# A gathered sum over edges: TensorE goes on by half batches, each behind VectorE's adds

## The chip, the cores and the metric

The kernel runs on one core of one Trainium2 chip. The metric is the device time of one execution, in microseconds (us). The engines are TensorE (PE for matmuls, PEld for weight loads in the profile), VectorE (DVE), ScalarE (ACT), GpSimd (POOL) and SyncE (SP); DMA engines move data between memory and the core.

## What is computed

Four graph layers follow each other on 6250 nodes with 256 features and 100000 edges: two attention layers (GAT and a second form), a transformer-like attention layer, and a graph convolution (GCN) with two convolutions. After each layer its result is added to the input and normalized. The change touches the two convolutions of the last layer, in the reference:

```python
def gcn_conv(x, src, dst, W, b, n):
    h = x @ W
    ...
    msg = h[s] * norm[:, None]
    out = jax.ops.segment_sum(msg, d, num_segments=n)
    return out + b
```

Here `segment_sum` adds up, for every node, the rows of the nodes that have an edge to it. The first convolution has rows of 128 numbers, the second rows of 64.

## The kernel before

The edges are sorted by their target and cut into 832 groups of 128 edges (`NSLOT`), so that all targets of a group lie in one window of 128 nodes. Eight groups are one batch, so a pass over the edges has 104 batches (`NBT`). There are six such passes: four for the attention layers (stages a1e, a2e, be and te in the profile) and two plain sum passes, g1e and g2e, made by `sum_pass` (L1856) with rows of 128 and of 64 numbers.

A sum pass works in this way, batch by batch (t):

- GpSimd (`gather`, L1889) fetches for each of the eight groups the 128 rows of the sources from the table in memory by an indirect DMA, L1893. Its destination is a ring of `RING` = 6 batches. It may fetch batch t once batch t - 6 has been summed (`s_summed`). Each half of a batch (four groups) has a semaphore of its own that tells of the landing.
- ScalarE (`mark`, L1920) makes for each group a 128 x 128 matrix of zeros and ones that says which edge goes to which node of the window: eight activations with Abs (L1923) and one with Relu over the whole batch (L1926), into one of `MARKS` = 4 buffers. It waits until that buffer's former batch has been summed.
- TensorE (`step`, L1902) multiplies each group's matrix by its rows, L1909, in float32. The profile shows two weight loads and two matmuls for each of the eight, so 16 and 16 for a batch. The eight results lie side by side in one of `AHEAD` = 4 buffers of PSUM. TensorE waits for the matrix, for the adds of the batch that had the same PSUM buffer (four batches back), and for the landing of each half. Its last matmul of a batch signals `s_summed`.
- VectorE (`step`, L1936) waits for that signal and adds the eight results to the accumulator in SBUF, each in the window of its group, L1943; each add signals `s_added`. The windows' places come from registers that are loaded for four batches at a time (L1061).

In g2e a part of the dense stage that follows is done beside the sums (class `Beforehand`, L1816): every second batch TensorE also transposes a window of x, ScalarE copies it, TensorE multiplies it by weights, and VectorE copies the product away. The engines' programs are written out batch after batch, in that order; nothing is planned at run time.

Of the kernel before, what the change touches and what calls it, by code (L numbers as in the profile page):

```python
# [1855 lines left out]
def sum_pass(nc, c, stage, order, table, width, acc, spare, beforehand=None):  # L1856
# [3 lines left out]
    RING, AHEAD, MARKS, U = 6, 4, 4, 4  # L1860
    with ExitStack() as stack:
# [19 lines left out]
        with nc.Block() as block:  # L1881
# [5 lines left out]
            @block.gpsimd  # L1887
            def _(pool):
                def gather(t):  # L1889
                    r = t % RING  # L1890
                    wait(pool, s_summed, t - RING + 1)
                    for k in range(8):
                        pool.indirect_dma_start(  # L1893
                            out=rows[:, r, k, :], out_offset=None, in_=table,
                            in_offset=bass.IndirectOffsetOnAxis(ap=order.row[:, t * 8 + k:t * 8 + k + 1], axis=0),
                        ).then_inc(s_rows[r][k // 4], 16)

                batches(pool, gather)

            @block.tensor  # L1900
            def _(pe):
                def step(t):  # L1902
                    r, u, b = t % RING, t % AHEAD, t % MARKS
                    pe.wait_ge(s_onehot, t + 1)
                    wait(pe, s_added, (t - AHEAD + 1) * 8)
                    for k in range(8):
                        if k % 4 == 0:
                            pe.wait_ge(s_rows[r][k // 4], t // RING * 64 + 64)
                        last = pe.matmul(ps_u[u][:, k * width:(k + 1) * width], onehot[b][:, k, :], rows[:, r, k, :], start=True, stop=True)  # L1909
                    last.then_inc(s_summed, 1)  # L1910
                    if window_at(t, 0) is not None:
# [7 lines left out]
            def _(act):  # L1919
                def mark(t):  # L1920
# [3 lines left out]
                    act.wait_ge(s_distance, t * 8 + 8)  # L1924
                    wait(act, s_summed, t - MARKS + 1)
                    act.activation(onehot[t % MARKS][:, :, :], distance[:, :, :], ACT.Relu, scale=-1.0, bias=1.0).then_inc(s_onehot, 1)  # L1926
# [6 lines left out]
            def _(dve):  # L1933
                windows = Windows(nc, order, mybir.EngineType.DVE, -8, U)

                def step(t):  # L1936
                    if t == 0:
                        return
                    dve.wait_ge(s_summed, t)
                    for k in range(8):  # L1940
                        mine = acc[:, bass.ds(windows.at(t % U, k - 8) * width, width)]
                        wait(dve, s_added, t * 8 + (k - 8))
                        dve.tensor_tensor(mine, mine, ps_u[(t - 1) % AHEAD][:, k * width:(k + 1) * width], ALU.add).then_inc(s_added, 1)  # L1943
# [1015 lines left out]
```

## Time and profile before

| what | value |
|---|---|
| median of 3 runs | 10409.85 us (10393.64 to 10424.56) |
| the profiled execution's own time | 10424.9 us |
| its span, from first to last instruction | 10423.2 us |
| mean granted TensorE clock | 0.706 of full speed |
| busy: TensorE matmul / VectorE / GpSimd / ScalarE | 6055.0 / 5838.2 / 5885.3 / 4570.6 us |
| g1e, first to last matmul | 7880.2 to 9062.1 us |
| g2e, first to last matmul | 9128.9 to 10316.2 us |

The profile is of one execution. Times are counted from the span's first instruction. Busy time is the time in which an engine works on an instruction; matmuls are pipelined, and the ends of their records are modelled. Idle time of an engine stands before the instruction that it waited for, with what ended the wait, as far as semaphores tell. "issue" means that nothing in the profile ended it. The granted clock is 0.50 (1.2 GHz) or 1.00 (2.4 GHz) at any moment; a figure between is a mean over a stretch.

### The profile page before, as it was taken

How to read it: one execution, taken by the hardware profiler on the slowest of the kernel's cores; microseconds unless marked ns; L12 is line 12 of the kernel's file. 1: busy time of each engine (PE TensorE's matmuls, PEld its weight loads, DVE VectorE, ACT ScalarE, POOL GpSimd, SP SyncE). 2: the span in 40 equal slices, each digit the busy share in tenths (PEclk: the TensorE clock that was granted, in tenths of full speed). 3: DMA queues.
4: the chain of work that ended last, by engine and by line, in shares of the span. 5: the costliest groups of instructions: out<-in, count | busy, mean ns of one | idle time of the engine just before them, and what ended most of it. 6: DMA issues, size and time to landing. Idle time of an engine off the chain costs nothing. (4 is left out here: it accounts for less than half of the span.)

```text
span 10423.2 us, 138279 instructions
## 1 busy us (share of the span) xinstructions
PE 6055.0 (58%) x32739; PEld 4141.4 (40%) x32739; DVE 5838.2 (56%) x17354; ACT 4570.6 (44%) x14076; POOL 5885.3 (56%) x6036
## 2 busy tenths in 40 slices
PE   5775566666556656565555567888873323333434
PEld 3443344444433333343333334555553222323333
DVE  8997566666555555564544568899982212211113
ACT  6996222222344444443222226777753323223332
POOL 7996455554444444425666615666655666466664
PEclk8998666666566666667666688899886555555556
DMA  1332333332222222223333325666641111111111
GB/s 52 117 105 87 107 100 98 97 99 82 61 64 64 66 74 64 62 68 103 107 107 106 107 90 167 177 181 181 179 132 45 47 46 47 40 26 23 23 24 37
DMA packets 518562, 902.79 MB, mean 87 GB/s; under 512 B 149378, under 2 KB 258844, under 8 KB 517404
## 3 DMA queue, kind: packets, MB, share of 16 engines
q0 software_dynamic: 226304, 550.69, 20.1%
q1 hardware_dynamic: 291484, 343.26, 10.8%
q8 instruction: 305, 5.00, 0.2%
q14 instruction: 469, 3.84, 0.1%
HBM read 820.41 MB, written 73.07 MB: 86 GB/s over the span
## 5 line engine op out<-in xcount | busy, mean ns | idle before, releaser
L1263 POOL DMA_INDIRECT all_Y<-table,all_row x3328 | 3212.0, 965 | 2817.5 <-DVE all_Y L1546 1482.1
L1893 POOL DMA_INDIRECT all_Y<-table,all_row x1664 | 1570.0, 943 | 825.0 <-issue 488.2
L1318 PE MATMUL be_ps_u<-all_Y,be_onehot 128*128 128x258 f32 x1664 | 669.8, 539 | 511.3 <-issue 260.9
L1909 PE MATMUL g1e_ps_u<-all_Y,g1e_onehot 128*128 128x128 f32 x1664 | 364.4, 351 | 830.7 <-issue 746.0
L1318 PE MATMUL a1e_ps_u<-all_Y,a1e_onehot 128*128 128x264 f32 x1664 | 788.1, 609 | 48.6 <-DVE all_acc L1558 47.6
L1943 DVE TENSOR_TENSOR all_acc<-all_acc,g1e_ps_u 128x128 f32 x832 | 238.8, 287 | 966.8 <-DMA all_window<-kept_window_dst 745.9
L1558 DVE TENSOR_TENSOR all_acc<-all_acc,be_ps_u 128x258 f32 x832 | 350.8, 422 | 604.2 <-remote 395.2
L1318 PEld LDWEIGHTS be_ps_u<-all_Y,be_onehot 128*128 128x128 f32 x1664 | 377.5, 258 | 755.0 <-issue 650.1
L1909 PEld LDWEIGHTS g1e_ps_u<-all_Y,g1e_onehot 128*128 128x128 f32 x1664 | 317.5, 261 | 877.6 <-issue 810.2
L1318 PE MATMUL te_ps_u<-all_Y,te_onehot 128*128 128x264 f32 x1664 | 586.6, 463 | 97.1 <-DVE all_Y L1538 59.8
L1943 DVE TENSOR_TENSOR all_acc<-all_acc,g2e_ps_u 128x64 f32 x832 | 183.5, 221 | 817.9 <-DMA table<-g2l_tile 383.1
L1318 PE MATMUL a2e_ps_u<-all_Y,a2e_onehot 128*128 128x66 f32 x1664 | 375.8, 363 | 448.7 <-DVE all_acc L1558 344.9
L1909 PE MATMUL g2e_ps_u<-all_Y,g2e_onehot 128*128 128x64 f32 x1664 | 309.8, 325 | 481.7 <-issue 454.5
L717 ACT ACTIVATE all_X<-all_Y,all_acc 128x128 f16<-128x128 f16 x784 | 239.6, 387 | 718.6 <-DVE all_acc L701 660.7
L747 PE MATMUL a2e_rank_ps_p<-all_X 128*128 128x512 f16 (+1 forms) x1568 | 545.2, 509 | 1.1 <-issue 0.9
L1297 PE MATMUL te_ps_q<-all_X,te_turned 128*128 x1664 | 490.1, 432 | 65.6 <-DVE te_product L1601 42.2
L1318 PEld LDWEIGHTS a2e_ps_u<-all_Y,a2e_onehot 128*128 128x128 f32 x1664 | 312.4, 262 | 515.5 <-issue 499.2
L649 POOL TENSOR_SCALAR all_acc<-all_Y,all_acc 128x128 f16<-128x128 f16 x392 | 488.8, 1258 | 45.4 <-DVE all_acc L636 35.4
L1909 PEld LDWEIGHTS g2e_ps_u<-all_Y,g2e_onehot 128*128 128x128 f32 x1664 | 313.0, 259 | 490.1 <-issue 471.1
L1318 PEld LDWEIGHTS a1e_ps_u<-all_Y,a1e_onehot 128*128 128x128 f32 x1664 | 424.1, 288 | 139.8 <-DVE all_Y L1546 52.1
L1484 ACT ACTIVATE be_onehot<-be_distance 128x1024 f32<-128x1024 f16 x104 | 109.9, 1057 | 842.0 <-PE be_ps_u L1318 739.2
L1926 ACT ACTIVATE g1e_onehot<-g1e_distance 128x1024 f32<-128x1024 f16 x104 | 109.9, 1057 | 815.5 <-DMA all_window<-kept_window_dst 752.0
(568 smaller groups left out, 16478.9 us busy)
## 6 DMA issues: line engine op xcount, KB each, us to landing
all_Y<-table,all_row POOLq DMA_INDIRECT x4992
a1e_place_row<-places_dst SPq DMA_DIRECT2D x104, 256.0 KB
a2e_place_row<-places_dst SPq DMA_DIRECT2D x104, 256.0 KB
be_place_row<-places_src SPq DMA_DIRECT2D x104, 256.0 KB
te_place_row<-places_src SPq DMA_DIRECT2D x104, 256.0 KB
all_Y<-lows_dst SPq DMA_DIRECT2D x98, 256.0 KB
all_Y<-codes_dst SPq DMA_DIRECT2D x98, 256.0 KB
all_acc<-lows_src SPq DMA_DIRECT2D x98, 256.0 KB
```

Of the source, the lines that this page charges most:

```text
L649: pool.tensor_scalar(self.row1[b][:, k, :], self.kept.half16, self.row[b][:, k:k + 1], self.kept.other_t[:, t * 8 + k:t * 8 + k + 1], ALU. ...
L717: act.activation(self.row1[b][:, k, :], self.kept.half16, ACT.Sign, bias=self.row[b][:, k:k + 1]).then_inc(self.s_valued, 1)
L747: last = pe.matmul(ps[:, 0:a1 - a0], self.row1[b][:, k, :], self.column1[b][:, k, a0:a1], start=first, stop=final)
L1263: pool.indirect_dma_start(out=rows[:, r, k, :], out_offset=None, in_=table, in_offset=bass.IndirectOffsetOnAxis(ap=order.row[:, t * 8 + k: ...
L1297: last = pe.matmul(ps_q[pair % 2][:, j * HC:(j + 1) * HC], turned[b][:, k * P:(k + 1) * P], queries[:, bass.ds(windows.at(windows_j, chunk ...
L1318: pe.matmul(ps_u[k % 4][:, 0:R], onehot[b][:, k, :], rows[:, t % RING, k, WEIGHT0:value_c0 + HC] if dot else summand[:, b, k, :], start=Tr ...
L1484: act.activation(onehot[b][:, :, :], distance[:, :, :], ACT.Relu, scale=-1.0, bias=1.0).then_inc(s_onehot, 1)
L1558: dve.tensor_tensor(mine, mine, ps_u[k % 4][:, 0:R], ALU.add).then_inc(s_added, 1)
L1893: pool.indirect_dma_start(out=rows[:, r, k, :], out_offset=None, in_=table, in_offset=bass.IndirectOffsetOnAxis(ap=order.row[:, t * 8 + k: ...
L1909: last = pe.matmul(ps_u[u][:, k * width:(k + 1) * width], onehot[b][:, k, :], rows[:, r, k, :], start=True, stop=True)
L1926: act.activation(onehot[t % MARKS][:, :, :], distance[:, :, :], ACT.Relu, scale=-1.0, bias=1.0).then_inc(s_onehot, 1)
L1943: dve.tensor_tensor(mine, mine, ps_u[(t - 1) % AHEAD][:, k * width:(k + 1) * width], ALU.add).then_inc(s_added, 1)
```

## The change

TensorE no longer waits for the batch four back. Before each half of a batch (four groups) it waits until all groups ahead of that half have been added, then for the half's landing, and it signals after each half. VectorE waits for each half's signal before its four adds. `s_summed` thus counts halves, and the waits of GpSimd and ScalarE on it count twice as many; they still stand for whole batches. Buffers, the number of matmuls, adds and gathers, and the work beside the sums in g2e stay the same.

```diff
             def _(pool):
                 def gather(t):
                     r = t % RING
-                    wait(pool, s_summed, t - RING + 1)
+                    wait(pool, s_summed, (t - RING + 1) * 2)
...
                     r, u, b = t % RING, t % AHEAD, t % MARKS
                     pe.wait_ge(s_onehot, t + 1)
-                    wait(pe, s_added, (t - AHEAD + 1) * 8)
-                    for k in range(8):
-                        if k % 4 == 0:
-                            pe.wait_ge(s_rows[r][k // 4], t // RING * 64 + 64)
-                        last = pe.matmul(ps_u[u][:, k * width:(k + 1) * width], onehot[b][:, k, :], rows[:, r, k, :], start=True, stop=True)
-                    last.then_inc(s_summed, 1)
+                    for half in range(2):
+                        wait(pe, s_added, t * 8 + half * 4)
+                        pe.wait_ge(s_rows[r][half], t // RING * 64 + 64)
+                        for k in range(half * 4, half * 4 + 4):
+                            last = pe.matmul(ps_u[u][:, k * width:(k + 1) * width], onehot[b][:, k, :], rows[:, r, k, :], start=True, stop=True)
+                        last.then_inc(s_summed, 1)
...
                     act.wait_ge(s_distance, t * 8 + 8)
-                    wait(act, s_summed, t - MARKS + 1)
+                    wait(act, s_summed, (t - MARKS + 1) * 2)
...
                     if t == 0:
                         return
-                    dve.wait_ge(s_summed, t)
                     for k in range(8):
+                        if k % 4 == 0:
+                            dve.wait_ge(s_summed, (t - 1) * 2 + (k // 4 + 1))
                         mine = acc[:, bass.ds(windows.at(t % U, k - 8) * width, width)]
```

## Rows read from the trace of the kernel before

**Rows 1.** Page, costliest groups: line engine op, out<-in, xcount | busy, mean ns | idle, releaser.

```profile
L1893 POOL DMA_INDIRECT all_Y<-table,all_row x1664 | 1570.0, 943 | 825.0 <-issue 488.2
L1909 PE MATMUL g1e_ps_u<-all_Y,g1e_onehot 128*128 128x128 f32 x1664 | 364.4, 351 | 830.7 <-issue 746.0
L1943 DVE TENSOR_TENSOR all_acc<-all_acc,g1e_ps_u 128x128 f32 x832 | 238.8, 287 | 966.8 <-DMA all_window<-kept_window_dst 745.9
```

**Rows 2.** Line L1893 (gathers): what ended POOL's idle time before it, us, times.

```profile
  issue: 488.2, 1589
  DMA all_window<-kept_window_dst: 145.2, 41
  PE g2e_ps_u L1909: 112.0, 25
  DMA table<-g2l_tile: 37.3, 7
```

**Rows 3.** Tiles g1e_ps_u, g2e_ps_u, be_ps_u: count, min/median/max ns, first and last start.

```profile
L1909 PE MATMUL g1e_ps_u<-all_Y,g1e_onehot x1664: 269/371/583, 7880.2 to 9062.1; 128*128 128x128 f32 x185
L1909 PE MATMUL g2e_ps_u<-all_Y,g2e_onehot x1664: 215/275/476, 9128.9 to 10316.2; 128*128 128x64 f32 x185
L1318 PE MATMUL be_ps_u<-all_Y,be_onehot x1664: 378/508/772, 4773.2 to 6059.8; 128*128 128x258 f32 x185
```

**Rows 4.** Timeline, POOL in g1e: start us, us, instruction [idle before <-releaser].

```profile
8462.45 0.94 POOL L1893 DMA_INDIRECT all_Y<-table,all_row  x1 [5.72 <-DMA all_window<-kept_window_dst]
...
8501.14 0.94 POOL L1893 DMA_INDIRECT all_Y<-table,all_row  x1 [0.31 <-issue]
8507.80 0.94 POOL L1893 DMA_INDIRECT all_Y<-table,all_row  x1 [5.73 <-DMA all_window<-kept_window_dst]
```

**Rows 5.** Timeline, VectorE (DVE) in the same stretch of g1e.

```profile
8462.32 3.29 DVE L1943 TENSOR_TENSOR all_acc<-all_acc,g1e_ps_u 128x128 f32 x8 [12.18 <-DMA all_window<-kept_window_dst]
8467.68 3.30 DVE L1943 TENSOR_TENSOR all_acc<-all_acc,g1e_ps_u 128x128 f32 x8 [2.06 <-issue]
8471.18 1.58 DVE L1943 TENSOR_TENSOR all_acc<-all_acc,g1e_ps_u 128x128 f32 x4 [0.21 <-issue]
```

**Rows 6.** Timeline, TensorE (PE) in the same stretch of g1e.

```profile
8461.42 7.76 PE L1909 MATMUL g1e_ps_u<-all_Y,g1e_onehot 128*128 128x128 f32 x44 [0.33 <-issue]
...
8473.88 0.37 PE L1909 MATMUL g1e_ps_u<-all_Y,g1e_onehot 128*128 128x128 f32 x1 [1.78 <-issue]
...
8506.78 1.50 PE L1909 MATMUL g1e_ps_u<-all_Y,g1e_onehot 128*128 128x128 f32 x4 [0.33 <-issue]
```

**Rows 7.** Timeline, TensorE at the start of g1e: batch 0's second half, then batch 1.

```profile
7885.25 2.08 PE L1909 MATMUL g1e_ps_u<-all_Y,g1e_onehot 128*128 128x128 f32 x8 [2.98 <-DMA all_Y<-table,all_row]
7890.25 2.04 PE L1909 MATMUL g1e_ps_u<-all_Y,g1e_onehot 128*128 128x128 f32 x8 [2.92 <-DMA all_Y<-table,all_row]
7895.20 2.07 PE L1909 MATMUL g1e_ps_u<-all_Y,g1e_onehot 128*128 128x128 f32 x8 [2.91 <-DMA all_Y<-table,all_row]
```

**Rows 8.** Timeline, VectorE at the start of g1e: the adds of batches 0, 1, 2.

```profile
7887.47 3.30 DVE L1943 TENSOR_TENSOR all_acc<-all_acc,g1e_ps_u 128x128 f32 x8 [16.96 <-PE g1e_ps_u L1909]
7921.64 3.29 DVE L1943 TENSOR_TENSOR all_acc<-all_acc,g1e_ps_u 128x128 f32 x8 [30.88 <-DMA all_window<-kept_window_dst]
7961.54 3.30 DVE L1943 TENSOR_TENSOR all_acc<-all_acc,g1e_ps_u 128x128 f32 x8 [36.61 <-DMA all_window<-kept_window_dst]
```

**Rows 9.** Line L1909 by stretch: us, PE busy (x) PEld busy (x), PEclk, DMA share, GB/s.

```profile
7897.30:7921.60 24.30, 8.35 (x31) 7.06 (x32) 0.50 0.20 51
7921.60:7961.50 39.90, 5.67 (x16) 4.61 (x17) 0.50 0.17 44
```

**Rows 10.** Timeline of the attention pass be: TensorE's sums, a gather, VectorE's next add.

```profile
5325.54 3.14 PE L1318 MATMUL be_ps_u<-all_Y,be_onehot 128*128 128x258 f32 x8
...
5333.35 0.95 POOL L1263 DMA_INDIRECT all_Y<-table,all_row  x1 [0.30 <-issue]
...
5334.67 0.42 DVE L1558 TENSOR_TENSOR all_acc<-all_acc,be_ps_u 128x258 f32 x1 [6.97 <-remote]
```

## The prediction

> **What bounds the kernel now.** The change touches one function, so I read the two stages that it makes, g1e and g2e, and leave the other 8,100 us alone: no instruction there is edited. First the costliest groups [rows 1]: the gather's line L1893 keeps GpSimd (POOL) busy for 1570.0 us and idle for 825.0 us; the sums of g1e are 364.4 us of TensorE and its adds 238.8 us of VectorE, both with more idle time than work. Then what ended POOL's idle time [rows 2]: 488.2 us is the 0.30 us between one gather and the next; 145.2 + 112.0 + 37.3 = 294.5 us in 73 waits is POOL standing before a ring slot that has not been summed (the two rows that name a DMA stand for the same wait, since the DMA named was long over). So the pace of a pass is eight gathers of 0.94 + 0.30 us, about 10.0 us for a batch, plus pauses. The first and last matmul of each pass [rows 3] give 1181.9 / 104 = 11.36 us for a batch in g1e and 1187.3 / 104 = 11.42 in g2e, 11.39 on the mean. The timeline of GpSimd [rows 4] shows the pause: 5.72 us, then 32 gathers, then 5.73 us: 45.35 us for four batches.
>
> Why is a slot not summed in time? TensorE's work in a cycle is small: 44 matmul records in a burst of 7.76 us, and then single records 2 to 3 us apart, each with idle time that nothing in the profile ends [rows 6]. The start of the pass tells more. There the matmuls come with the data, 5 us apart [rows 7], and the batch-0 sums, whose last matmuls begin as a group at 7885.25, are added from 7887.47 on [rows 8]. Batch 1's last matmuls run from 7895.20 to 7897.3, but VectorE, idle for 30.88 us, adds them only from 7921.64, and batch 2's from 7961.54. So the sums are done long before the signal of them arrives. Between batch 1's last matmul and its add TensorE took 31 matmuls and 32 weight loads, and in the next 39.9 us 16 and 17 [rows 9]. From this I take a rule of this kernel: while POOL gathers without a break, some number of TensorE instructions are signalled at once, and after that one for each gather. The counts: 64 instructions (two batches of 16 loads and 16 matmuls) by 7921.6, in 41.4 us or 33 gathers, so 31 free ones; then 33 in 39.9 us or 32 gathers. A pause of POOL clears it: after 8501.14 POOL stands still and the burst comes back at about 8506.8 [rows 4, 6]. The pass paces itself in this way: POOL runs ahead until the ring is full, stops, and TensorE's signals come.
>
> The Trainium skill (Perfetto Trace Analysis, Tensor Engine Instruction) says that a matmul's end in the trace is worked out and that its semaphore goes out only when PSUM has acknowledged the write. The trace agrees that the two may differ: under 0.2 us for batch 0, 24 us for batch 1.
>
> **The change part by part.**
> (a) Signals per half, POOL's and ScalarE's waits doubled in count: 104 more increments in each pass, and both still wait for whole batches. Nothing by itself; ScalarE's work for a batch hides in 10 us as before.
> (b) VectorE may add four sums as soon as the half is signalled. The adds (0.43 us apart, eight in 3.30 us, four in 1.58 us [rows 5]) are the same in number. Nothing is saved where POOL sets the pace, as it waits for the end of a batch.
> (c) TensorE's new wait: before a half, all earlier sums must be added. Behind it on TensorE's queue stand that half's 16 loads and matmuls, and in g2e every second batch the transposes and product of the dense stage; for these wait ScalarE's copy and VectorE's keep, and for the sums POOL. A half then costs, from first load to first add, 7887.47 - 7885.25 = 2.22 us [rows 7, 8], plus 1.58 us of adds, plus some 0.1 us from the last add to TensorE's next load (estimated from VectorE's end at 8467.68 + 3.30 = 8470.98, with adds of the next batch 0.2 us behind [rows 5]): 3.9 us at the granted clock of 0.50 (1.2 GHz) that this stretch had [rows 9] and that I keep; 7.8 us for a batch, and with a quarter of the 2.06 us in which VectorE loads its windows [rows 5] 8.3 us. That is less than the gathers' 10.0, so with prompt signals the wait is hidden. Its cover is gone in a pause: what TensorE now does in a burst for nearly three batches, it must then do at 3.9 us a half, and nothing is finished ahead that a pause could signal at once.
>
> The cycle by the rule: POOL resumes when batch m is signalled, with 31 free instructions. Batch m+1 needs 32, is through in 8.3 us, and POOL goes straight on to its second batch, up to 20.0 us. Batch m+2 needs 64 in all; 31 + 16 gathers give 47, so at 20 us about one half of it is through, and POOL stops. The pause: from 0.3 us (in be, the gather of 5333.35 ends at 5334.3 and the add comes at 5334.67 [rows 10]) to 4.7 us (g1e, from 8502.1 to 8506.8 [rows 4, 6]) until signals flow, and then 3.9 to 5.6 us for the half that is left, the latter if the first half's adds are still to come. So 4.2 to 10.3 us of pause behind 20 us: 12.1 to 15.1 us a batch. If some 17 more instructions are free, three batches go between pauses: (30 + 4.2) / 3 = 11.4 to (30 + 10.3) / 3 = 13.4. The ends are 11.4 and 15.1, middle 13.25. The nearest row is the attention pass be, where TensorE is held to a few sums ahead of VectorE: its matmuls span 1286.6 us [rows 3], 12.37 us a batch, and there too VectorE stands idle for 6.97 us in a run of gathers although four sums were computed from 5325.54 to 5328.7 [rows 10]. So holding TensorE back does not free the signals. I take 12.6, nearer to that row.
>
> Sum: 12.6 - 11.39 = 1.21 us, times 208 batches, 252 us. The profiled execution took 10424.9 us, 15 above the median of the runs shown, so 10677 by the profile and 10662 beside the median: I say 10660.
>
> **The rivals.**
> A, faster (chance 0.27). The crawl comes from TensorE's own backlog: it runs up to four batches ahead, its unsignalled instructions pile up, and with at most 16 outstanding they never do. For it: batch 0, with nothing ahead of it, was signalled promptly in the midst of gathers, and batch 1's signal came after 63 further records [rows 8, 9]. Against it: batch 1 too had nothing unsignalled ahead of it, and be's stall has only eight matmuls outstanding [rows 10]. It decides if a lone half is signalled in a run of gathers; then all 294.5 us of POOL's pauses [rows 2] go: 10424.9 - 294.5 - 15 = 10115. The Trainium skill (TensorE: Matmul & The Clock Gate, Architectural detail) gives TensorE a queue of 64 instructions, in which weight loads may pass matmuls. By that page a wait that keeps the queue short would keep it from ever filling; the 63 records agree with such a depth, and the time by it would be rival A's.
> B, no change (0.09): the free instructions are enough for four batches and the pause stays at 5.7 us; 45.4 us for four batches as now, 10410.
> C, far slower (0.05): a half is signalled only in a pause, so that each batch has its own: 10.0 + 4.7 + 3.9 = 18.6 us, 7.2 x 208 = 1500 us more, 11910.
>
> **How the numbers follow.** The forecast has 0.59, with 11.9 to 13.6 us a batch: 106 to 460 us more, 10515 to 10870. Slower by over 0.3% (about what a measurement of this kernel tells from no change) is the forecast and C, less its lowest edge: 0.63. Rival A gives faster, 0.28 with what lies between it and B; same is 0.09. The range leaves out C, the forecast's top, and A's full gain, and reaches down into a partial gain: 10180 to 10860.
>
> **What would show it.** Right: in the middle of g1e POOL pauses every two or three batches, for 5 to 10 us; VectorE's adds come in fours; between them it idles over 5 us while the matmuls of the half have long ended; TensorE's bursts hold 8 records, never 44. The sum of POOL's pauses on L1893 rises from 294.5 to about 550 us. Wrong: POOL at 1.25 us a gather all through with no pauses (A), or pauses of unchanged number and length (B). The forecast falls if a half's adds start within about 2.3 us of its first load throughout the runs of gathers.

## The result, and the profile after

The changed kernel takes 10529.9 us (median of 4 runs, 10514.7 to 10542.9) against 10409.4 for the kernel before: a ratio of 1.0119, 95% interval 1.0102 to 1.0136, or 120.5 us more. The forecast was 252 us more. The direction was right; the size was about twice too large.

Both matmul tiles of the passes, after (answering to [rows 3]; columns: count, min/median/max ns, first and last start):

```profile
L1909 PE MATMUL g1e_ps_u<-all_Y,g1e_onehot x1664: 421/421/583, 7842.3 to 9143.2; 128*128 128x128 f32 x185
L1909 PE MATMUL g2e_ps_u<-all_Y,g2e_onehot x1664: 219/421/476, 9197.5 to 10413.6; 128*128 128x64 f32 x185
```

g1e takes 1300.9 us, 12.51 a batch where the forecast had 12.6; g2e takes 1216.1 us, 11.69 a batch. So in these profiles the passes lost 119.0 and 28.8 us. The profiled executions are 10514.7 and 10424.9 us, 89.8 apart; the 58.0 us between that and the passes' 147.8 are elsewhere, in code that is the same: the first matmul of g1e came 37.9 us earlier here, and over all profiles of this case, whose code up to g1e is the same too, it lies anywhere between 7842 and 7988 us.

The costliest groups of the passes, after (answering to [rows 1]): the adds work as long as before, the sums 428.7 us where it was 364.4, POOL's idle time has grown.

```profile
L1893 POOL DMA_INDIRECT all_Y<-table,all_row x1664 | 1569.9, 943 | 927.4 <-issue 473.8
...
L1909 PE MATMUL g1e_ps_u<-all_Y,g1e_onehot 128*128 128x128 f32 x1664 | 428.7, 439 | 883.8 <-DVE all_acc L1944 461.3
L1944 DVE TENSOR_TENSOR all_acc<-all_acc,g1e_ps_u 128x128 f32 x832 | 238.6, 287 | 1074.3 <-DMA all_window<-kept_window_dst 645.7
```

What ended POOL's idle time before its gathers, after (answering to [rows 2]):

```profile
  issue: 473.8, 1550
  PE g1e_ps_u L1909: 204.2, 31
  DMA table<-g2l_tile: 144.4, 46
  DMA all_window<-kept_window_dst: 47.3, 33
...
  PE g2e_ps_u L1909: 17.0, 2
```

Without "issue", and without the one wait at the start of each pass, these are 412.9 us where 294.5 stood before. Now the middle of g1e after, POOL (gathers that follow a pause; the others come 0.30 us apart), VectorE and TensorE (answering to [rows 4 to 6]):

```profile
8467.38 0.94 POOL L1893 DMA_INDIRECT all_Y<-table,all_row  x1 [7.48 <-PE g1e_ps_u L1909]
...
8488.73 0.94 POOL L1893 DMA_INDIRECT all_Y<-table,all_row  x1 [1.67 <-DMA all_window<-kept_window_dst]
...
8504.53 0.94 POOL L1893 DMA_INDIRECT all_Y<-table,all_row  x1 [6.12 <-PE g1e_ps_u L1909]
```

```profile
8467.25 1.57 DVE L1944 TENSOR_TENSOR all_acc<-all_acc,g1e_ps_u 128x128 f32 x4 [2.28 <-PE g1e_ps_u L1909]
8471.12 1.57 DVE L1944 TENSOR_TENSOR all_acc<-all_acc,g1e_ps_u 128x128 f32 x4 [2.29 <-issue]
8474.98 1.58 DVE L1944 TENSOR_TENSOR all_acc<-all_acc,g1e_ps_u 128x128 f32 x4 [2.28 <-issue]
8478.85 1.57 DVE L1944 TENSOR_TENSOR all_acc<-all_acc,g1e_ps_u 128x128 f32 x4 [2.30 <-PE g1e_ps_u L1909]
8488.60 1.58 DVE L1944 TENSOR_TENSOR all_acc<-all_acc,g1e_ps_u 128x128 f32 x4 [8.18 <-DMA all_window<-kept_window_dst]
8500.55 1.57 DVE L1944 TENSOR_TENSOR all_acc<-all_acc,g1e_ps_u 128x128 f32 x4 [10.37 <-DMA all_window<-kept_window_dst]
8504.40 1.58 DVE L1944 TENSOR_TENSOR all_acc<-all_acc,g1e_ps_u 128x128 f32 x4 [2.27 <-PE g1e_ps_u L1909]
```

```profile
8480.48 2.08 PE L1909 MATMUL g1e_ps_u<-all_Y,g1e_onehot 128*128 128x128 f32 x8 [1.78 <-DVE all_acc L1944]
8490.28 2.05 PE L1909 MATMUL g1e_ps_u<-all_Y,g1e_onehot 128*128 128x128 f32 x8 [7.72 <-issue]
8502.18 2.07 PE L1909 MATMUL g1e_ps_u<-all_Y,g1e_onehot 128*128 128x128 f32 x8 [9.85 <-DVE all_acc L1944]
```

The reader is to see three things. Adds come in fours, 3.86 us apart while signals are prompt (forecast: 3.9). The half summed from 8480.48 to 8482.56 is added only at 8488.60, the next only at 8500.55: late signals, with no crawl of single records, since TensorE may not run ahead. And POOL gathers 16, stops 1.67 us, gathers 8, stops 6.12 us: 37.15 us for three batches, 12.4 a batch. The sums run at the granted clock that the forecast kept, 0.50 (1.2 GHz), by the row of 400 us of g1e (columns as in [rows 9], with the other engines between):

```profile
8200.00:8600.00 400.00, 134.01 (x520) 115.78 (x520) 75.55 (x264) 113.45 (x291) 242.45 (x257) 0.50 0.16 42
```

In the kernel before, the same 400 us had a mean of 0.57, with 0.69 in the stretch from 8461 to 8470 us that holds a burst: there a part ran at 1.00 (2.4 GHz). With the bursts that is gone, and the sums of g1e grew from 364.4 to 428.7 us. It is not what the change costs: spacer_each below has 0.50 there too and takes what the kernel before takes.

In g2e it looks different. POOL and VectorE after:

```profile
9718.01 0.94 POOL L1893 DMA_INDIRECT all_Y<-table,all_row  x1 [3.16 <-DMA table<-g2l_tile]
...
9740.83 0.94 POOL L1893 DMA_INDIRECT all_Y<-table,all_row  x1 [3.16 <-DMA table<-g2l_tile]
...
9763.62 0.94 POOL L1893 DMA_INDIRECT all_Y<-table,all_row  x1 [3.12 <-DMA table<-g2l_tile]
```

```profile
9717.88 1.31 DVE L1944 TENSOR_TENSOR all_acc<-all_acc,g2e_ps_u 128x64 f32 x4 [5.02 <-DMA table<-g2l_tile]
...
9725.21 1.31 DVE L1944 TENSOR_TENSOR all_acc<-all_acc,g2e_ps_u 128x64 f32 x4 [2.17 <-PE g2e_ps_u L1909]
9727.75 0.42 DVE L1853 COPY all_acc<-g2e_ps_o 128x256 f32<-128x256 f32 x1 [1.23 <-issue]
9732.97 1.31 DVE L1944 TENSOR_TENSOR all_acc<-all_acc,g2e_ps_u 128x64 f32 x4 [4.80 <-DMA table<-g2l_tile]
9740.70 1.31 DVE L1944 TENSOR_TENSOR all_acc<-all_acc,g2e_ps_u 128x64 f32 x4 [6.42 <-DMA table<-g2l_tile]
```

A pause of 3.16 us behind every 16 gathers, 47 times in the pass, and no more: when POOL stops, both halves of the batch that it waits for are computed, and only the last signal is owed. My two-batch cycle had a pause of at least 4.2 us here and 10.3 at most.

### The profile page after: what moved, and what is told of

The parts are those of the page before. It is cut to its first block and busy times, and to the rows that moved or that the text cites. A ratio compares the mean times of both kernels' runs of the same rounds, so it can differ in the third digit from the quotient of the medians.

```text
span 10513.0 us, 138695 instructions
## 1 busy us (share of the span) xinstructions
PE 6163.2 (59%) x32739; PEld 4225.8 (40%) x32739; DVE 5847.3 (56%) x17354; ACT 4568.3 (43%) x14076; POOL 5883.5 (56%) x6036
## 3 DMA queue, kind: packets, MB, share of 16 engines
q14 instruction: 471, 3.86, 0.1%
## 5 line engine op out<-in xcount | busy, mean ns | idle before, releaser
L1893 POOL DMA_INDIRECT all_Y<-table,all_row x1664 | 1569.9, 943 | 927.4 <-issue 473.8
L1909 PE MATMUL g1e_ps_u<-all_Y,g1e_onehot 128*128 128x128 f32 x1664 | 428.7, 439 | 883.8 <-DVE all_acc L1944 461.3
L1909 PE MATMUL g2e_ps_u<-all_Y,g2e_onehot 128*128 128x64 f32 x1664 | 381.8, 407 | 702.1 <-DVE all_acc L1944 445.0
L1909 PEld LDWEIGHTS g1e_ps_u<-all_Y,g1e_onehot 128*128 128x128 f32 x1664 | 370.5, 328 | 941.9 <-DVE all_acc L1944 491.3
L1909 PEld LDWEIGHTS g2e_ps_u<-all_Y,g2e_onehot 128*128 128x128 f32 x1664 | 361.6, 316 | 748.0 <-DVE all_acc L1944 462.5
```

The costliest lines, as they stand in the source:

```text
L1893: pool.indirect_dma_start(out=rows[:, r, k, :], out_offset=None, in_=table, in_offset=bass.IndirectOffsetOnAxis(ap=order.row[:, t * 8 + k: ...
```

## The experiments

Ratios are to the kernel before on the same chip, whose median was 10508, 10511, 10528, 10512 and 10384 us in the five sessions. All kernels in one table; the spans are from the first to the last matmul of a pass, by 104 batches; a pause is a gap of over 0.8 us between two gathers in POOL's timeline (the memsets of the later kernels are in it), and the usual ones are given, with the number of gathers ahead of each. A kernel with a time in place of the ratio ran once. In first_ring_only, two_of_four, sp_loads, uncoupled and half_rows some of the work is left out, or rows are summed that are not the edges'.

| kernel | time, ratio (95%) | g1e, g2e us a batch | usual pauses in g1e; g2e, us |
|---|---|---|---|
| before | 1 | 11.36, 11.42 | 1.5 to 3.0 behind 24, then 3.0 to 4.4 behind 8, or 5.7 behind 32; 4.5 behind 24 |
| changed | 1.0119 (1.0102 to 1.0136) | 12.51, 11.69 | 1.0 or 1.7 behind 16, then 4.7 to 7.5 behind 8, or 8.1 behind 24; 3.1 behind 16 |
| after_again | 1.008 (1.0054 to 1.0106) | 11.98, 11.90 | 3.2 behind 16, or 2.5 behind 16 and 2.5 behind 8, or 1.8 and 5.5; 3.3 to 4.7 behind 16 |
| wait_alone | 1.0032 (1.0020 to 1.0044) | 11.66, 11.70 | 3.2 behind 16, or 1.8 to 2.5 behind 16 and 2.5 to 3.1 behind 8; 3.3 behind 16 |
| g1e_only | 1.0049 (1.0030 to 1.0068) | 11.94, 11.53 | as after_again; 4.7 behind 24 |
| halves_old_wait | 0.9996 (0.9983 to 1.0009) | 11.40, 11.48 | 4.5 behind 24; 4.7 behind 24 |
| first_ring_only | 9744 us | 8.14, 7.26 | no gathers |
| two_of_four | 10544 us | 11.49, 11.64 | 3.6 behind 32, 3.7 behind 8; 4.5 behind 24 |
| sp_loads | 9621 us | 7.72, 6.85 | no gathers |
| spacer2 | 1.0156 (1.0120 to 1.0191) | 12.17, 12.38 | 4.1 to 7.3 behind 24; 3.5 behind 16, or 7.6 behind 24 |
| quarters | 1.0173 (1.0149 to 1.0198) | 11.81, 12.84 | 3.2 behind 16; 4.4 to 7.1 behind 16 |
| slot_halves_old | 0.9999 (0.9987 to 1.0010) | 11.41, 11.49 | 4.5 behind 24; 4.7 behind 24 |
| ring12 | 1.0017 (1.0004 to 1.0030) | 11.44, 11.64 | 3.7 behind 8, 2.5 behind 24; 4.7 behind 24 |
| spacer_each | 10529 us | 11.49, 11.49 | none; none |
| after_space64 | 1.0138 (1.0121 to 1.0155) | 12.62, 11.94 | 7.4 behind 24, or 0.8 behind 16 and 7.3 behind 8; 3.0 behind 16 |
| after_space128 | 1.0118 (1.0101 to 1.0135) | 11.83, 12.27 | 2.9 behind 24; 2.8 to 6.5 behind 24 |
| before_space128 | 0.9997 (0.9988 to 1.0007) | 11.47, 11.51 | 1 to 3; 3.6 behind 32 |
| before_space192 | 1.0008 (0.9992 to 1.0023) | 11.42, 11.52 | 3.1 behind 64; 2.9 behind 48 |
| uncoupled | 11476 us | 16.86, 16.52 | see below |
| half_rows | 10572 us | 11.73, 12.91 | 3.8 behind 16; 6.5 behind 16 |

**Which part costs.** Session one takes the change apart.

**wait_alone**, on the kernel before:

```diff
-                    wait(pe, s_added, (t - AHEAD + 1) * 8)
+                    wait(pe, s_added, t * 8)
```

> The kernel before with the strict wait alone: one signal and eight adds per batch as before, but TensorE starts a batch only when all sums ahead of it are added. Theory (signals come late while POOL gathers, and the strict wait leaves nothing finished that a pause could signal at once): as slow as the change or slower, since a whole batch of 3.7 us of sums and 3.3 us of adds is owed in a pause; g1e 12.5 to 14 us a batch, g2e 11.5 to 13, 10550 to 10750 us, say 10620. Rival (the halves, that is the signal and the separate wait per four sums, are what costs): within 30 us of the kernel before, 10410.

1.0032: less than the theory's least. A whole batch late costs hardly more than a half late: from first sum to first add 11.0 us on the mean in g1e, against 9.4 for a late half of the changed kernel. Late, that is added over 1 us after the last sum, were 64 of g1e's 104 batches, and 69 of its 208 halves in the changed kernel.

**g1e_only**, on the changed kernel (`H` is 2 where the width is 128, else 1, and takes the place of the factor 2):

```diff
-                        wait(pe, s_added, t * 8 + half * 4)
+                        wait(pe, s_added, t * 8 + half * 4 if H == 2 else (t - AHEAD + 1) * 8)
```

> The change in g1e alone; g2e keeps whole-batch signals and the old wait. Theory: in the profile of the changed kernel g1e's matmuls span 119 us more and g2e's 29 us more, so nearly all of the +120 is here: 10490 to 10530 us, g2e back at 11.4 us a batch. Rival (the two passes share the loss, and the differing profiles of one execution each mislead): about 10470, with g1e near 11.9 us a batch.

1.0049, or 51 us more, with g1e at 11.94 and not 12.51 a batch, though its code is that of the changed kernel. That is the rival's guess (60 us more, 11.9 a batch) and not the theory's. The same code has more than one rhythm.

**halves_old_wait**, on g1e_only:

```diff
-                        wait(pe, s_added, t * 8 + half * 4 if H == 2 else (t - AHEAD + 1) * 8)
+                        wait(pe, s_added, (t - AHEAD + 1) * 8)
```

> In g1e alone: signals and adds per half as in the change, but TensorE keeps the old wait (up to four batches ahead); g2e as before. Theory (the wait is the cause): no loss, 10380 to 10425 us, g1e at 11.2 to 11.5 us a batch, bursts of some 44 matmul records and crawls as before. Rival (the halving costs): as with the change in g1e, about 10500.

0.9996, as expected: in g1e signals and adds per half cost nothing. The strict wait costs, and in g1e more with halves (11.94 and more a batch) than with batches (11.66). In g2e halves with the old wait were not tried.

**first_ring_only**, on the changed kernel:

```diff
-                batches(pool, gather)
+                batches(pool, gather, RING)
...
-                        pe.wait_ge(s_rows[r][half], t // RING * 64 + 64)
+                        pe.wait_ge(s_rows[r][half], 64)
```

> The changed kernel, but in both passes only the first six batches are gathered; all later batches sum the rows that lie in the ring, so 2 x 784 gathers are left out, the sums and adds stay. Theory (POOL's gathers make the signals late): every half is signalled promptly, first load to last add 3.9 us as in my step (c), 7.8 to 8.3 us a batch in g1e and less in g2e: the passes 860 and 800 us, the program near 9670 us. Rival (the exchange between TensorE and VectorE is itself the price, or signals come late with TensorE's own backlog): VectorE still idles 5 us and more before some halves, and the passes stay above 10 us a batch, 10250 to 10530 us.

g1e at 8.14 us a batch: the forecast's 8.3 for the exchange without gathers was well sized. Late signals need POOL's gathers.

**What makes a signal late.** Session two.

**after_again** is the changed kernel, unaltered.

> The changed kernel once more, beside the kernel before on the same chip. With the change in g1e alone, g1e's matmuls spanned 1242 us where the whole change had 1301, though the code of that pass is the same, so the length of the pauses may differ from run to run or from chip to chip. Theory: the pass falls into one of two rhythms, with pauses of 3.2 us behind 16 gathers (11.7 us a batch) or of 6 to 8 us where a half is still owed (12.5), and which one is a matter of fractions of a microsecond; then the ratio lies anywhere from 1.004 to 1.012 and g1e's span between 1215 and 1301 us, g2e's 1216 again. Rival (the ratio is a property of the code): 1.010 to 1.014 and 1290 to 1310 us again.

1.008, g1e at 1245.7 us: within the theory's span for g1e, though g2e, at 1237.1, was 21 us longer than in the first profile. What the change costs in one profile is good to about 55 us a pass.

**two_of_four** (and the adds of the two sums left out read the other two's columns):

```diff
-                        for k in range(half * 4, half * 4 + 4):
+                        for k in range(half * 4, half * 4 + 2):
```

> The changed kernel with two of the four matmuls of each half left out (the adds read the other two sums' columns instead, so adds, gathers and waits stay in number). Theory (late signals are counted in TensorE's instructions: some 48 free after a pause, then one for each gather): a batch has 16 instructions instead of 32 and 8 are signalled per batch of gathers, so a pause comes only after 48 / 8 = 6 batches instead of 2, and at about 3.2 us each the pauses fall from 250 and 161 us to about 55 in each pass: 10.5 us a batch, the program 150 to 300 us under the changed kernel beside it. Rival (signals come late by time or by half, not by instruction): the pauses stay behind every 16 gathers, over 140 us in each pass, and the time within 80 us of the changed kernel's.

The theory missed: the pauses fell only to 148 us in g1e, and stayed at 164 in g2e. VectorE in a run of gathers:

```profile
8704.06 1.58 DVE L1944 TENSOR_TENSOR all_acc<-all_acc,g1e_ps_u 128x128 f32 x4 [1.44 <-issue]
8711.64 1.58 DVE L1944 TENSOR_TENSOR all_acc<-all_acc,g1e_ps_u 128x128 f32 x4 [6.00 <-DMA all_window<-kept_window_dst]
8722.83 1.58 DVE L1944 TENSOR_TENSOR all_acc<-all_acc,g1e_ps_u 128x128 f32 x4 [9.61 <-DMA all_window<-kept_window_dst]
```

Halves of half the size are late all the same, though the runs grew from 16 gathers to 32 in g1e and 24 in g2e. So when lateness begins is not a count of TensorE's instructions alone; the fixed number of "free instructions" of my rule falls.

**sp_loads** (POOL's block is gone, the landing waits count 16 instead of 64):

```diff
+                    for half in range(2):
+                        a = (t * 2 + half) % 12 * 512
+                        sp.dma_start(rows[:, r, half * 4:half * 4 + 4, :], table[a:a + 512].rearrange("(k p) n -> p k n", p=P)).then_inc(s_rows[r][half], 16)
```

> The changed kernel with POOL's gathers replaced by two plain loads a batch that SyncE issues: the same bytes in packets of the same size into the same slots, but consecutive rows of the table. Theory (it is POOL's issuing of gathers that makes the signals late, not the bytes that arrive): every half prompt, as with the first ring only: g1e 8.1 to 8.4 us a batch, g2e 7.3 to 7.6, the program 730 to 790 us under the kernel before. Rival (the traffic into SBUF makes TensorE's signals late): VectorE waits over 5 us in runs of loads, over 9.5 us a batch in both passes.

7.72 us a batch and every half prompt (2.28 us of idle VectorE, the wait of a prompt half above). It is the gathers, not the bytes. What of the gathers it is, this run does not tell: the trace has the loads' bytes in packets of 512 bytes where a gather's come in packets of 4096 (so they were not of the same size), and 32 increments of a landing's semaphore in a batch where the gathers make 128.

**spacer2**, ahead of each batch's eight gathers:

```diff
+                    for i in range(t * 2, t * 2 + 2):
+                        wait(pool, s_space, i)
+                        pool.memset(space[:, :], 0.0).then_inc(s_space, 1)
```

> The changed kernel with two small POOL memsets, some 0.3 us each, ahead of each batch's gathers, so that the run of gathers is broken for about 1 us in each batch. Theory (what clears the signals is POOL not gathering for about 3 us): a break of 1 us clears nothing or a few instructions, pauses stay behind 16 gathers, and the 208 breaks cost up to 1 us each less what they take from the pauses: 30 to 200 us over the changed kernel. Rival (any gap lets waiting signals through, as the 0.30 us between gathers lets one): the pauses shrink by more than the breaks add, and the time falls by 30 to 150 us below the changed kernel's.

About 87 us above after_again (10680.4 to 10593.2), as the theory had it. But in g1e nearly every long pause came behind 24 gathers, where after_again had them behind 16 too, which no theory had said.

**Rate or price.** Session three.

**quarters** (waits, signals and adds by two; the two other waits count times four):

```diff
-                        wait(pe, s_added, t * 8 + half * 4)
+                        wait(pe, s_added, t * 8 + part * 2)
```

> The change made finer: TensorE signals, and VectorE adds, per two sums instead of four, and TensorE goes on to the next two only when all ahead are added. In a run of gathers a late signal costs 9 to 11 us from first sum to first add for a whole batch of 32 TensorE instructions (the strict wait alone), 9 us on the mean for a half of 16 (the change), 6 to 8 us for a half of 8 (two sums of four left out). Theory (a late signal has its price, nearly whatever it covers): from about 13 us after POOL resumes each quarter costs 6 to 7 us, so that a quarter or two are owed when the ring is full; pauses of 5 to 8 us behind 16 gathers, 12.5 to 13.5 us a batch in both passes, 1.02 to 1.04 of the kernel before. Rival (late signals go by the instruction, as my rule had it): four quarters cost what two halves cost, 1.006 to 1.013.

1.0173, between the two. A late quarter takes 5.0 us from first sum to first add, a late half 9, a late batch 11: neither by the signal alone nor by the instruction alone. g1e fell into the rhythm of 3.2 us behind 16 gathers and was faster than the changed kernel's; the theory had 5 to 8 us there.

**slot_halves_old**, on halves_old_wait:

```diff
-                    wait(pool, s_summed, (t - RING + 1) * H)
                     for k in range(8):
+                        if k % (8 // H) == 0:
+                            wait(pool, s_summed, (t - RING) * H + k // 4 + 1)
```

> In g1e alone: signals and adds per half with the old wait (as in the kernel that matched the kernel before), and POOL also waits per half: it gathers the first four rows of a slot as soon as that half of the slot is summed. g2e as before. Theory (about 3.1 us of POOL's pause are the time until the late signals come, the rest of the 4.5 us is the second half of the batch): pauses of about 3.2 us behind 24 to 32 gathers instead of 4.5, 0.3 to 0.5 us a batch less in g1e, 0.995 to 0.998 of the kernel before. Rival (POOL resumes before all owed signals are out, and the next run starts late already): runs of 4 to 12 gathers and as much pause in all, or more, 1.000 to 1.010.

0.9999, nothing gained: where POOL resumed sooner, the next pause came sooner.

**ring12**, on the kernel before:

```diff
-    RING, AHEAD, MARKS, U = 6, 4, 4, 4
+    RING, AHEAD, MARKS, U = 6 * (128 // width), 4, 4, 4
```

> The kernel before with a ring of twelve batches in g2e, whose rows are half as wide (g1e keeps six). Theory (signals are prompt for some 13 us after a pause, in which TensorE can sum four batches if they have been gathered; a fuller ring gives it more to sum): runs of 32 to 40 gathers between pauses of 4.5 us instead of 24, 10.9 to 11.1 us a batch in g2e, 30 to 55 us less, 0.995 to 0.997. Rival (what TensorE gets through in a cycle is set by the dense stage's copies and by the four batches that it may be ahead, not by what lies in the ring): runs of 24 gathers and 4.5 us, 0.999 to 1.001.

1.0017: only the first run grew (120 gathers, then 15.6 us). Both kernels that should have saved pauses saved none.

**spacer_each**, ahead of each gather:

```diff
+                        wait(pool, s_space, t * 8 + k)
+                        pool.memset(space[:, :], 0.0).then_inc(s_space, 1)
```

> The changed kernel with one small POOL memset ahead of each gather, some 0.27 us by the kernel that had two of them a batch, so that gathers come every 1.5 us instead of 1.25. Theory (something fills while gathers come faster than it drains, and signals are late when it is full): at 1.5 us it fills more slowly or not at all, runs are longer than 16 gathers or there is no pause, 12.2 us a batch or little more in both passes. Rival (time or count since the last pause alone decides): pauses of 3 us and more still behind 16 gathers, 13.7 us a batch and more, with the first late half some 13 us, or 12 gathers, behind each pause.

This run turned the case. With gathers 1.44 us apart there is not one pause, and in g1e not one late half. First what ended POOL's idle time before its memsets, in both passes as a whole, then VectorE in g1e:

```profile
L1895 POOL MEMSET all_Y<- x1664: 311/325/338, 7967.6 to 10419.7; 128x256 f32 x185
its engine sat idle before it (us, times) until:
  POOLq L81: 38.7, 2
```

```profile
8508.44 1.57 DVE L1947 TENSOR_TENSOR all_acc<-all_acc,g1e_ps_u 128x128 f32 x4 [4.15 <-PE g1e_ps_u L1912]
8513.85 1.58 DVE L1947 TENSOR_TENSOR all_acc<-all_acc,g1e_ps_u 128x128 f32 x4 [3.84 <-PE g1e_ps_u L1912]
```

VectorE idles while the next half's rows come in, four gathers of 1.44 us; its add follows the half's first sum by 2.2 us on the mean. And the program takes 10529 us, what the kernel before takes beside it: POOL loses in the memsets what it had lost in pauses. The two idle entries are the passes' starts. In g2e, however, 70 of the 208 halves are still added over 1 us after their last sum, by up to 5.9 us; with the loads of sp_loads none is by more than 0.5. They come in time for POOL.

**What the pace is made of.** Session four varies the interval, on the changed kernel and on the one before.

**after_space64**, **after_space128**, **before_space128**, **before_space192**: the edit of spacer_each with 64, 128 or 192 columns, on the kernel that the name says.

```diff
-        space = spare[:, RING * 8 * width:RING * 8 * width + 256]
+        space = spare[:, RING * 8 * width:RING * 8 * width + 128]
```

> The changed kernel with a memset of 64 columns ahead of each gather, some 0.15 us, so that gathers come about every 1.26 us (0.94 of the gather, 0.17 ahead of it, 0.15) where the changed kernel has 1.25. Theory (the rate of the gathers decides, somewhere between 1.25 and 1.44 us): nearly the changed kernel's time, pauses behind 16 to 24 gathers, 1.00 to 1.015 of the kernel before. Rival (any POOL instruction between two gathers lets the signals through, whatever the rate): no pauses, 10.1 us a batch, 0.975 to 0.98.

> The same with 128 columns, some 0.21 us: gathers every 1.32 us, 10.6 us a batch. Theory (rate), where the limit is under 1.32: no pauses in g1e and hardly any in g2e, every half of g1e prompt at some 2.2 us from first sum to first add, both passes 10.6 us a batch, 160 us under the kernel before, 0.983 to 0.988. Where the limit is above 1.32: runs longer than 16 gathers and pauses of 3 to 6 us, 11.3 to 12.3 us a batch, 0.998 to 1.02.

> The kernel before (whole batches, TensorE up to four batches ahead) with the same memset of 128 columns ahead of each gather. Theory (the rate of the gathers is the cause, and the waits of the change only decide what a late signal costs): as fast as the changed kernel with the same memset, within 0.3%, at 0.983 to 0.988, if the limit is under 1.32 us; TensorE's sums come in bursts of 16 records and crawl nowhere. Rival (the strict wait is what keeps TensorE's queue short enough to be signalled at this rate): crawls and pauses stay, 1.00 to 1.015, while the changed kernel with the memset is faster.

> The kernel before with a memset of 192 columns ahead of each gather, some 0.27 us: gathers every 1.38 us, 11.0 us a batch. Theory (rate): no pauses and no crawl, 0.990 to 0.994 of the kernel before, slower than with 128 columns if that one has no pauses either. Rival (the old wait needs pauses at any rate): 11.0 and 1.4 us of pause a batch, 1.015 to 1.025.

With 64 columns the changed kernel kept its pauses, so it is not any instruction between that helps. With 128 the limit turned out to lie above (1.0118, as the second case of its expectation had it), and the kernel before was not faster for it (0.9997): both of its expectations missed. With 192 columns the kernel before took 1.0008, between its two expectations, and its POOL pauses so (memsets that follow a pause, 64 gathers 1.39 us apart between):

```profile
8503.66 0.26 POOL L1895 MEMSET all_Y<- 128x192 f32 x1 [2.77 <-DMA all_window<-kept_window_dst]
...
8595.39 0.26 POOL L1895 MEMSET all_Y<- 128x192 f32 x1 [2.79 <-DMA all_window<-kept_window_dst]
```

64 gathers in 91.73 us are 1.433 each. Now lay the rows side by side: 32 gathers and 5.7 us of pause at 1.25 us are 45.35 / 32 = 1.417 [rows 4]; in g2e after, 16 gathers and 3.16 us are 22.8 / 16 = 1.426; here 1.433; at 1.44 no pause. In these, at three intervals and with either wait, a gather takes 1.42 to 1.44 us on the mean, and the pause gives back what the run ahead of it had gained: 0.17 to 0.18 us for each gather at 1.25. I call this the debt. It is the least that a pass pays, and not always all of it: from the first gather to the last, g1e of the changed kernel has 1.529 us a gather and g2e of quarters 1.56, because there more than the last signal is owed when POOL stops.

**Whose pace.** Session five frees POOL from the sums, and halves the rows.

**uncoupled** (TensorE uses slots 0 to 2 and waits for their first landing):

```diff
-                    r = t % RING
-                    wait(pool, s_summed, (t - RING + 1) * 2)
+                    r = t if t < 3 else 3 + t % 3
                     for k in range(8):
+                        if k % 4 == 0:
+                            wait(pool, s_rows[r][k // 4], (t // 3 - 1) * 64 if t >= 3 else 0)
```

> The changed kernel with gathers and sums freed of each other: TensorE sums the first three batches of rows over and over, and POOL gathers all later batches into the other three slots of the ring, where it waits only until its own gather of three batches before has landed (the sums use rows that are not theirs; every instruction stays). Theory (a debt of the gathers: each needs 1.41 to 1.45 us, though POOL can issue one every 1.25): POOL waits for the landing from some point of the pass on, its 832 gathers of a pass still span 1170 to 1200 us, and TensorE's signals are late for stretches of many halves, since no pause of POOL clears them. Rival (the pauses are made by TensorE's late signals): POOL issues all through at 1.25 us, 1040 us a pass, and the program is 230 to 290 us under the kernel before.

POOL waited for almost nothing (0.6 us for landings), but its gathers came hardly faster: the first 188 come 1.26 us apart, and after them they take 144 to 147 us for 104 gathers, 1.39 to 1.42 each, because some gathers themselves grow longer (start, us):

```profile
8815.58 0.94 POOL L1894 DMA_INDIRECT all_Y<-table,all_row  x1 [0.30 <-issue]
8816.83 1.80 POOL L1894 DMA_INDIRECT all_Y<-table,all_row  x1 [0.30 <-issue]
8818.93 1.80 POOL L1894 DMA_INDIRECT all_Y<-table,all_row  x1 [0.30 <-issue]
8821.03 1.09 POOL L1894 DMA_INDIRECT all_Y<-table,all_row  x1 [0.30 <-issue]
8822.43 1.09 POOL L1894 DMA_INDIRECT all_Y<-table,all_row  x1 [0.30 <-issue]
8823.83 0.95 POOL L1894 DMA_INDIRECT all_Y<-table,all_row  x1 [0.31 <-issue]
```

TensorE meanwhile gets one half of g1e through in 22.40 us, early in the pass, where POOL still issues every 1.25 us, and late:

```profile
7919.26 1.58 DVE L1948 TENSOR_TENSOR all_acc<-all_acc,g1e_ps_u 128x128 f32 x4 [20.82 <-DMA all_window<-kept_window_dst]
7941.66 1.58 DVE L1948 TENSOR_TENSOR all_acc<-all_acc,g1e_ps_u 128x128 f32 x4 [20.82 <-issue]
...
8860.06 1.58 DVE L1948 TENSOR_TENSOR all_acc<-all_acc,g1e_ps_u 128x128 f32 x4 [20.82 <-DMA all_window<-kept_window_dst]
8882.46 1.58 DVE L1948 TENSOR_TENSOR all_acc<-all_acc,g1e_ps_u 128x128 f32 x4 [20.82 <-issue]
...
9007.06 1.58 DVE L1948 TENSOR_TENSOR all_acc<-all_acc,g1e_ps_u 128x128 f32 x4 [12.41 <-DMA all_window<-kept_window_dst]
9010.93 1.58 DVE L1948 TENSOR_TENSOR all_acc<-all_acc,g1e_ps_u 128x128 f32 x4 [2.29 <-PE g1e_ps_u L1913]
```

22.40 us are 16 times 1.40: one TensorE instruction for each 1.40 us, whether POOL issues a gather in that time or somewhat more. The other half of my rule, one instruction for each gather, is so shown for a POOL that never stops, with 1.40 us in the place of the 1.25 that I had. The kernel before has the same beat. Where its TensorE crawls, single matmuls start 2.80 us apart, each 1.40 us behind a weight load (8480.19, 8482.98):

```profile
8478.78 0.37 PE L1909 MATMUL g1e_ps_u<-all_Y,g1e_onehot 128*128 128x128 f32 x1 [2.42 <-issue]
8481.59 0.37 PE L1909 MATMUL g1e_ps_u<-all_Y,g1e_onehot 128*128 128x128 f32 x1 [2.44 <-issue]
8484.38 0.37 PE L1909 MATMUL g1e_ps_u<-all_Y,g1e_onehot 128*128 128x128 f32 x1 [2.42 <-issue]
```

Nor are the rows late. In uncoupled's g1e the last of a gather's 16 packets of 4 bytes, as many as the increments on which its landing is waited for, is written 1.1 to 1.7 us after the gather instruction ends, for the last gathers as for the first. Yet behind POOL's last gather (8981.0) TensorE's signals stay late until the add at 9007.06, which is 832 times 1.40 us after the pass's first gather (7842.8). So something behind the gathers, and not the arrival of their rows, seems to be worked off at 1.40 us a gather; what it is, no run shows. Nor is the debt exact to the hundredth: at 1.40 us a gather the 64 gathers of before_space192 would owe under 1 us, and their pause is 2.8.

The theory's limit on the pace holds, though its place was missed: the span is 1138 us and not 1170 to 1200, since the first 188 gathers ran on credit, and the price is paid mostly in the gather, not in a wait. The program was 1092 us over the kernel before.

**half_rows**:

```diff
-                            out=rows[:, r, k, :], out_offset=None, in_=table,
+                            out=rows[0:64, r, k, :], out_offset=None, in_=table,
```

> The changed kernel with gathers of 64 rows instead of 128, into 64 of the 128 partitions (half of the rows that are summed are not gathered; all instructions stay in number). Theory (the debt is of the gather's rows): 0.7 us a gather, less than POOL's own pace, so no pauses, every half prompt at 2.2 us from first sum to first add, and POOL's own pace or the exchange of 7.3 to 8.1 us a batch sets the passes: 8.1 to 10.1 us a batch, 270 us or more under the kernel before. Rival (it is of the gather, whatever its rows, or of TensorE's signals): pauses as in the changed kernel, 11.4 to 12.5 us a batch.

The theory missed: with 64 rows the pauses stay (3.8 us behind 16 in g1e, 1189 us for the pass's gathers). In g1e the debt goes by the gather, not by its rows. The Trainium skill (DMA: Bandwidth & Descriptors, Why a DMA increments its semaphore by 16 and not by 1) says that for a DMA issued by GpSimd all 16 DMA engines post their increment, whatever the transfer's shape. The trace has 16 packets of 4 bytes for a gather, with 64 rows as with 128. A cost per gather agrees with that; no run here shows that it is this one. Why g2e was slower here, 6.5 us behind 16, stays open.

No kernel that does all of the work beats the kernel before. An estimate of what is left: 832 gathers at uncoupled's 1.39 to 1.40 us are 1156 to 1165 us a pass, where POOL's first to last gather spanned 1174 and 1177 us before, so some 20 to 40 us in all, and 75 by the 1138 us that uncoupled itself took.

## Why the prediction was right in sign and wrong in size

- *What bounds the passes.* I took "about 10.0 us for a batch, plus pauses", and the pauses for the effect of late signals alone. The runs show another floor: a gather's sustained pace is 1.39 to 1.44 us, 11.1 to 11.5 a batch. POOL can issue at 1.25 on credit, and pays in pauses, in longer gathers (uncoupled) or not at all if it is slowed to 1.44 (spacer_each). It is still the late signal that stops POOL, since left alone it issued 188 gathers at 1.26; but what such a stop costs was owed in the main. That the signals are late because of the debt is my reading: they are late in g1e where gathers come faster than 1.40 us, and prompt at 1.44. The profile before had the debt: [rows 2] 294.5 us of pauses by 1664 gathers are 0.177 us each, and [rows 4] give the same for one cycle.
- *Part (a) and (b): nothing by themselves.* Right where it was tried, in g1e (halves_old_wait, 0.9996).
- *Part (c): 3.9 us a half, 8.3 us a batch.* Right: 3.86 us in the trace, 8.14 a batch without gathers.
- *The cycle by the rule.* This step failed. Its rule of "31 free instructions, then one for each gather" holds only in its second half, with 1.40 us for a gather, and only while the debt stands. The free ones are not counted in instructions: half the instructions left pauses behind 24 to 32 gathers (two_of_four). So "at 20 us about one half of it is through" was wrong. In g2e the whole batch was through, and the pause was 3.16 us, under my least value of 4.2: 0.18 us for each of 16 gathers, by the reading above a debt that is paid in any case and in which the late signal hides.
- *The mis-sized term.* 12.6 - 11.39 = 1.21 us for each of 208 batches; the 120.5 us measured are 0.58. g1e came near it in the first profile (12.51), which is in part luck, as it had 11.98 in the second and 11.94 in g1e_only, where 24 gathers often ended with 5.0 us of pauses in all instead of 7.8; g2e had 11.69 and 11.90. I had carried over the pace of the attention pass be [rows 10], which no run shows to be the nearer case, to both passes. What the change costs is only what its exchange adds beside the debt: in g1e a half still owed when POOL has already stopped, the pauses of 4.7 to 8.1 us.
- *Rival A.* Its time of 10115 us was out of reach: in uncoupled, where POOL does not wait for the sums at all, a pass's gathers span 1138 us, 36 and 39 us less than before and not half of 294.5. Its cause falls too: in uncoupled, where at most 16 TensorE instructions are outstanding, each half takes 22.40 us. The Trainium skill (TensorE: Matmul & The Clock Gate, Architectural detail) has TensorE's queue at 64 instructions; keeping it short did not make the signals prompt. Rival B's unchanged pause did not come, nor C's pause in each batch.
- *What would show it.* Fours, bursts of 8, idle VectorE beside ended matmuls, and pauses behind two or three batches all came; the pauses' sum was 412.9 us and not 550, which is the same miss.

Open: what in the chip the gathers and TensorE's signals share, and why the same code falls into pauses of 3.2 us in one profile and of 8.1 in another.

## What to carry to other kernels

Before a pause is called a loss, divide it by the work of the run before it: if the quotient is the same for short and long runs, it may be a debt, and removing the wait then removes nothing. Test that: slow the supposed pacemaker by a few tenths of a microsecond and see whether the time moves. A tighter handshake costs little as long as it fits into a wait that is owed anyway (here 0.27 us a batch in g2e), so price it against that wait and not against zero.

## What the runs showed that I had not expected

- POOL's indirect gathers can be issued 1.25 us apart for some 188 in a row, but sustain 1.39 to 1.44 us, with 128 rows of 512 or 256 bytes.
- While gathers come faster than that, TensorE's signals come late, in the changed kernel by up to 25 us; with POOL never stopping, at one instruction for each 1.40 us (22.40 us for 16). The rows themselves land 1.1 to 1.7 us after each gather all the while (uncoupled, g1e).
- A pause of about 3 us makes them prompt again; breaks of 0.85 us did not (spacer2).
